# First attention: heads 8 to 15 of q turned in squares of 32 by VectorE and carried by transfers

## The chip, the core and the metric

The kernel runs on one core of a Trainium2 chip. The metric is the time of one execution on the device, in microseconds (us). A core has five engines that run side by side and wait for each other through semaphores: TensorE (PE; its loads of weights are PEld), VectorE (DVE), ScalarE (ACT), GpSimd (POOL) and SyncE (SP), which here only issues transfers (DMAs). TensorE runs at one of two clocks, 1.2 or 2.4 GHz; the profile gives the granted clock as a share of the higher.

## What is computed

Two transformer layers on 32 samples of 256 tokens by 128 features. The change is in the attention of the first layer, with 16 heads of q, 8 of k and v, 64 features a head:

```python
x = _rmsnorm(tokens, norm_w)
q = (x @ Wq).reshape(b, n, QH, DH).transpose(0, 2, 1, 3)
kv = x @ Wkv
...
q = _mh_rmsnorm(q, q_gamma)
k = _mh_rmsnorm(k, k_gamma)
g = QH // H
q = q.reshape(b, H, g, n, DH)
sim = jnp.einsum('bhgid,bhjd->bhgij', q, k)
sim = jnp.tanh(sim / SOFTCLAMP) * SOFTCLAMP
sim = sim * DH ** (-0.5)
...
attn = jax.nn.softmax(sim, axis=-1)
out = jnp.einsum('bhgij,bhjd->bhid', attn, v)
```

Before it stand a layer norm with a scale and a shift per sample, behind it a gated addition to x, then a mixture of experts, a second attention and a second feed-forward.

## The kernel before

Everything stays in the core's memory. `attention0` works sample by sample (n from 0 to 31); a sample is two tiles of 128 tokens (t = 0, 1). Each engine has its own order written out by hand in a loop over n, and a round of the loop mixes work of samples n - 1 to n + 3, so that the engines always have something of another sample.

For one sample: TensorE turns the normalised tokens (L314), projects q and k into three PSUM banks `pW` (L363, six blocks m = 0 to 5, f32), and v (L333). ScalarE squares each block (L761), VectorE multiplies it by a gain into `qg` (L582), sums the squares (L588), makes the factors (L603 to L622) and normalises (L629). Then q and k are split into two f16 halves, a high part by ScalarE (`act_hi`, L771) and the rest by `lower` (L643; k by VectorE, q by GpSimd), side by side in `kp` and `qp`, 64 + 64 columns a head. TensorE turns them, 128x128 at a time against the identity in `id16`: k in `pe_turn_k` (L375), q in `pe_turn_q` (L391), four groups i of eight heads (i = 2j + t, with j = 0 for heads 0 to 7 and j = 1 for heads 8 to 15). ScalarE copies k to `k1` (L777), VectorE q to `qs` (L651). SP copies `k1` with its halves exchanged to `k2` by two transfers (L306, L307).

The scores of a sample are four groups g of four heads (`pe_scores`, L407, eight matmuls each, called S0 to S3 in the text): q against `k1` and `k2`, summed in PSUM `pS`. S0 and S1 are heads 0 to 7, S2 and S3 heads 8 to 15. ScalarE takes tanh and exp of each group (L789, L795), GpSimd masks it (L864), TensorE multiplies by v for two heads at a time (`pe_weighted_values`, L422 and L423, p = 0 to 7), VectorE divides (L634, L638), GpSimd adds the two heads of a pair (L872). Pairs 6 and 7 of sample n - 1 are done after S0 of sample n. The turned heads go back through L444, L458 and L464 and are added to x.

Where q is turned in the order of the engines: i = 0 and 1 of sample n + 1 after S3 of sample n; i = 2 and 3 of sample n just after its S0, around pair 7 of sample n - 1. S0 waits for the copies of i = 0 and 1 and for `k2`, S2 for those of i = 2 and 3:

```python
if g == 0:
    pe.wait_ge(s_qs, 4 * n + 2)
    pe.wait_ge(s_k2, 32 * (n + 1))
elif g == 2:
    pe.wait_ge(s_qs, 4 * n + 4)
```

Of the kernel before, what the change touches and what calls it, by code (L numbers as in the profile page):

```python
# [241 lines left out]
def attention0(nc, c, weights):  # L242

    with ExitStack() as ctx:

# [3 lines left out]
        def sem(name):  # L251
# [8 lines left out]
        PAIRS = KH  # L260
        qp, kp = sb('qp', [P, TT, QH, 2 * DH], F16), sb('kp', [P, TT, KH, 2 * DH], F16)
        qs = [sb(f'qs{k}', [P, QH, N], F16) for k in range(2)]
        k1 = [sb(f'k1{k}', [P, KH, N], F16) for k in range(2)]
# [21 lines left out]
        BANK_OF = (0, 1, 2, 1, 0, 2)  # L285
        QT_BANK = (1, 0, 0, 2)
        SAMPLES_OF_LOAD = B // X_LOADS
# [3 lines left out]
            sem(x) for x in ('qk', 'sq', 'qg', 'ss', 'f', 'qn', 'hi', 'lo', 'ql'))  # L291
        s_qt, s_qs, s_kt, s_ks = (sem(x) for x in ('qt', 'qs', 'kt', 'ks'))
        s_k2, s_v, s_va = (sem(x) for x in ('k2', 'v', 'va'))
# [5 lines left out]
        @block.sync  # L299
        def _(sp):  # L300
            for n in range(B):
                k = n % 2
                if n >= 2:
                    sp.wait_ge(s_sc, 4 * (n - 1))
                sp.wait_ge(s_ks, 2 * n + 2)
                sp.dma_start(k2[k][0:DH, :, :], k1[k][DH:P, :, :]).then_inc(s_k2, 16)  # L306
                sp.dma_start(k2[k][DH:P, :, :], k1[k][0:DH, :, :]).then_inc(s_k2, 16)  # L307

        def pe_transpose_x(pe, n):
# [13 lines left out]
        def pe_values(pe, n, t):  # L323
            if t == 0:
                if n >= 1:
                    pe.wait_ge(s_qs, 4 * n)
                else:
                    pe.wait_ge(s_qg, 6)
            elif n + 1 < B:
                pe.wait_ge(s_qg, 6 * n + 7)  # L330
            else:
                pe.wait_ge(s_qs, 4 * n - 1)
            pe.matmul(pW[(2, 0)[t]][:, :], hT[n % 2][:, t * P:(t + 1) * P], wkv[:, KW:2 * KW], start=True, stop=True).then_inc(s_v, 1)  # L333

        def pe_project_qk(pe, n, m):
            if m == 0:
                pe.wait_ge(s_hT, n + 1)
                if n >= 2:
                    pe.wait_ge(s_qs, 4 * n - 5)
                elif n:  # L340
                    pe.wait_ge(s_qg, 5)
            elif m == 1:
                pe.wait_ge(s_msv, n + 1)
            elif m == 2:
                if n:
                    pe.wait_ge(s_va, 2 * n - 1)
            elif m == 3:
                if n:
                    pe.wait_ge(s_qs, 4 * n - 3)
                else:  # L350
                    pe.wait_ge(s_qg, 2)
            elif m == 4:
                if n:
                    pe.wait_ge(s_qs, 4 * n - 2)
# [22 lines left out]

        def pe_turn_q(pe, n, i):
            j, t = i // 2, i % 2
            if j == 0:  # L380
                pe.wait_ge(s_ql, 2 * n + t + 1)
                pe.wait_ge(s_ks, 2 * n + t + 1)
            elif n + 1 < B:
                pe.wait_ge(s_qg, 6 * n + 11 + t)
            elif t == 0:
                pe.wait_ge(s_qs, 4 * n + 2)
            else:
                pe.wait_ge(s_st, 4 * n - 7)
            out = pW[QT_BANK[i]][:, :].bitcast(F16)
            for h in range(KH):  # L390
                last = pe.transpose(out[:, h * P:(h + 1) * P], qp[:, t, j * KH + h, :], c.id16[:, :])  # L391
            last.then_inc(s_qt, 1)

        def pe_scores(pe, n, g):
            k = n % 2
            if g == 0:
                pe.wait_ge(s_qs, 4 * n + 2)
                pe.wait_ge(s_k2, 32 * (n + 1))
            elif g == 2:
                pe.wait_ge(s_qs, 4 * n + 4)  # L400
            if n or g:
                pe.wait_ge(s_th, 4 * n + g)
            for hh in range(0, HPG, G2):
                h = g * HPG + hh
                for out, keys in ((pS[:, hh * N:(hh + G2) * N], 0), (pS[:, HPG * N + hh * P:HPG * N + (hh + G2) * P], 1)):
                    for first, kk in ((True, k1[k]), (False, k2[k])):
                        last = pe.matmul(out, kk[:, h // G2, keys * P:(keys + 1) * P], qs[k][:, h:h + G2, keys * P:N], start=first, stop=not first)  # L407
            last.then_inc(s_sc, 1)
# [17 lines left out]
        def pe_heads_back(pe, n, t):  # L426
            if t == 0:
                pe.wait_ge(s_as, 8 * n + 8)
                if n + 3 < B:
                    pe.wait_ge(s_qg, 6 * n + 20)  # L430
                elif n + 3 == B:
                    pe.wait_ge(s_qg, 6 * B - 2)
                elif n + 2 == B:
                    pe.wait_ge(s_qs, 4 * B - 3)
                else:
                    pe.wait_ge(s_at, 2 * n - 1)
            elif n + 2 < B:
# [9 lines left out]
        def pe_out_project(pe, n):  # L447
            pe.wait_ge(s_at, 2 * n + 2)
            if n + 3 < B:
                pe.wait_ge(s_qg, 6 * n + 21)  # L450
            elif n + 3 == B:
                pe.wait_ge(s_va, 2 * B - 1)
            elif n + 2 == B:
                pe.wait_ge(s_qs, 4 * B)
            else:
                pe.wait_ge(s_st, 4 * n - 3)
# [116 lines left out]
        def dve_gain(dve, n, m):  # L573
# [66 lines left out]
        def lower(eng, n, u, t, done):  # L640
            eng.wait_ge(s_hi, 4 * n + 2 * u + t + 1)
            to, x = ((kp, qg[n % 2][:, t, QW:]), (qp, qg[n % 2][:, t, 0:QW]))[u]
            eng.tensor_tensor(to[:, t, :, DH:2 * DH], x.rearrange('p (h d) -> p h d', d=DH), to[:, t, :, 0:DH], ALU.subtract).then_inc(done, 1)  # L643

        def dve_take_q(dve, n, i):
            j, t = i // 2, i % 2
            dve.wait_ge(s_qt, 4 * n + i + 1)
            if i == 0 and n >= 2:
                dve.wait_ge(s_sc, 4 * n - 4)
            out = qs[n % 2][:, j * KH:(j + 1) * KH, t * P:(t + 1) * P]  # L650
            dve.tensor_copy(out, pW[QT_BANK[i]][:, :].bitcast(F16).rearrange('p (h i) -> p h i', i=P)).then_inc(s_qs, 1)  # L651

# [8 lines left out]
        def _(dve):  # L661
# [13 lines left out]
            for n in range(-3, B + 1):  # L675
# [7 lines left out]
                if 0 <= n < B:  # L683
                    dve_take_q(dve, n, 2)
                if 0 <= n + 1 < B:
# [3 lines left out]
                if 0 <= n < B:  # L689
                    dve_take_q(dve, n, 3)  # L690
                if 0 <= n + 1 < B:
# [71 lines left out]
        def act_hi(act, n, u, t):  # L763
            act.wait_ge(s_qn, 2 * n + t + 1)
            if n >= 1:
                if u:
                    act.wait_ge(s_qt, 4 * n - 1 + t)
                else:
                    act.wait_ge(s_kt, 2 * n - 1 + t)
            to, x = ((kp, qg[n % 2][:, t, QW:]), (qp, qg[n % 2][:, t, 0:QW]))[u]  # L770
            act.activation(to[:, t, :, 0:DH], x.rearrange('p (h d) -> p h d', d=DH), ACT.Copy).then_inc(s_hi, 1)  # L771

# [39 lines left out]
        def _(act):  # L812
# [3 lines left out]
            for n in range(-3, B + 1):  # L816
# [58 lines left out]
        def _(gp):  # L875
# [11 lines left out]
            for n in range(-1, B + 1):  # L887
# [1206 lines left out]
```

## Time and profile before

| | us |
|---|---|
| median of 3 runs | 2152.71 (2152.59 to 2153.12) |
| the profiled execution | 2151.95, its span 2150.1 |
| TensorE busy in the span | 2047.2 (95%) |
| VectorE, ScalarE, GpSimd busy | 1650.3 (77%), 1438.3 (67%), 618.3 (29%) |
| first attention, from the first scores to the last | 72.2 to 978.4 |

The profile is of one execution. Busy time is what an engine spent in instructions. A stretch is a piece of the span, given by its start and end. In the order of time a row is one group of like instructions of an engine, and square brackets behind it give the idle time before it and who ended it. Starts are in us from the start of the span.

### The profile page before, as it was taken

The numbers are of one execution on the slowest core, as the hardware profiler recorded it, in microseconds if no ns is written. First come the engines' busy times: TensorE is split into PE (matmuls) and PEld (weight loads), VectorE is DVE, ScalarE is ACT, GpSimd is POOL, SyncE is SP. The second block draws the span as 40 slices with busy tenths as digits, with TensorE's granted clock in tenths as the row PEclk, the third lists the DMA queues.
The fourth block names the chain that finished last, engine by engine and source line by source line (L and its number), as shares of the span: only waits on it lengthen the run. The fifth ranks groups of instructions, "written<-read, shape, count | busy, mean of one in ns | idle before, by whom it ended". The sixth has DMA issues, their size and how long they took to land. (4 is left out here: it accounts for less than half of the span.)

```text
span 2150.1 us, 40463 instructions
## 1 busy us (share of the span) xinstructions
PE 2047.2 (95%) x14885; PEld 1372.3 (64%) x14885; DVE 1650.3 (77%) x4015; ACT 1438.3 (67%) x1931; POOL 618.3 (29%) x862
## 2 busy tenths in 40 slices
PE   3899999999999999997999999799999996999998
PEld 1577777777777777775444444577777773444443
DVE  3888888888888888874566665577777776999997
ACT  1687877778887777873666666466666663555554
POOL 1345444544544454552000000133333331000000
PEclk9999999999999999997999999899999997999999
DMA  5000000000000000001000000000000000000000
GB/s 165 21 21 21 21 11 21 21 21 21 21 21 11 21 21 21 21 21 55 1 0 1 1 1 1 1 2 2 2 2 2 2 2 1 10 16 11 15 11 20
DMA packets 32834, 35.30 MB, mean 16 GB/s; under 512 B 6864, under 2 KB 26496, under 8 KB 32640
## 3 DMA queue, kind: packets, MB, share of 16 engines
q1 hardware_dynamic: 32640, 32.73, 5.8%
q8 instruction: 120, 1.97, 0.4%
q14 instruction: 74, 0.61, 0.1%
HBM read 11.75 MB, written 4.19 MB: 7 GB/s over the span
## 5 line engine op out<-in xcount | busy, mean ns | idle before, releaser
L864 POOL TENSOR_SCALAR_AFFINE_SELECT pr<-pr 128x512 f32<-128x512 f32 x256 | 202.2, 813 | 370.7 <-ACT pr L795 370.7
L422 PE MATMUL a_pO<-va,pr 128*128 128x66 f32 x2048 | 304.6, 272 | 1.9 <-POOL pr L864 1.5
L422 PEld LDWEIGHTS a_pO<-va,pr 128*128 128x128 f32 x2048 | 273.7, 193 | 18.9 <-issue 15.4
L1628 ACT ACTIVATE c_pr<-c_pS 128x1536 f32<-128x1536 f32 x128 | 186.0, 1453 | 119.3 <-PE c_pS L1440 119.3
L1683 POOL TENSOR_SCALAR_AFFINE_SELECT c_pr<-c_pr 128x512 f32<-128x512 f32 x256 | 158.0, 641 | 265.4 <-DVE c_pr L1548 265.4
L761 ACT ACTIVATE sq<-a_pW 128x512 f32<-128x512 f32 x192 | 114.4, 597 | 145.4 <-PE a_pW L363 142.7
L789 ACT ACTIVATE th<-a_pS 128x1536 f32<-128x1536 f32 x128 | 185.9, 1453 | 30.1 <-PE a_pS L407 29.6
L423 PE MATMUL a_pO<-va,pr 128*128 128x66 f32 x1024 | 199.0, 276 | 0.0
L795 ACT ACTIVATE pr<-th 128x1536 f32<-128x1536 f32 x128 | 190.5, 1488 | 3.1
L407 PE MATMUL a_pS<-qs,k 128*128 128x512 f16 (+1 forms) x1024 | 187.3, 326 | 0.9 <-issue 0.9
L1548 DVE TENSOR_SCALAR c_pr<-c_pr 128x1536 f32<-128x1536 f32 x128 | 122.6, 958 | 78.4 <-ACT c_pr L1628 78.4
L1021 PE MATMUL b_pU<-b_hT,b_uT 128*128 128x512 f32 x320 | 168.8, 610 | 0.0
L1039 PE MATMUL b_pD<-b_a,b_dT 128*128 128x512 f32 x320 | 163.1, 593 | 0.0
L407 PEld LDWEIGHTS a_pS<-qs,k 128*128 128x128 f16 x1024 | 98.7, 98 | 99.7 <-issue 35.9
L1187 DVE TENSOR_TENSOR b_a<-b_q,b_pC 128x512 f32<-128x512 f32 x128 | 87.8, 686 | 96.1 <-ACT b_q L1271 96.0
L1258 ACT ACTIVATE b_r<-b_pU 128x512 f32<-128x512 f32 x160 | 95.4, 596 | 95.6 <-PE b_pU L1021 95.6
L423 PEld LDWEIGHTS a_pO<-va,pr 128*128 128x128 f32 x1024 | 156.6, 193 | 0.0
L872 POOL TENSOR_TENSOR as<-on 128x128 f32<-128x128 f32 x256 | 116.6, 466 | 109.7 <-PE a_pW L444 95.0
L643 POOL TENSOR_TENSOR qp<-qg,qp 128x1024 f16<-128x1024 f32 x64 | 136.7, 2137 | 25.2 <-ACT qp L771 25.2
L582 DVE TENSOR_TENSOR qg<-a_pW,a_gam 128x512 f32<-128x512 f32 x192 | 131.4, 685 | 10.5 <-ACT sq L761 7.9
L634 DVE RECIPROCAL rl<-a_pO 128x4 f32<-128x4 f32 x256 | 45.0, 176 | 120.5 <-PE a_pO L423 120.5
L363 PE MATMUL a_pW<-a_wq,hT 128*128 128x512 f32 x256 | 125.7, 615 | 1.3 <-DVE qs L651 0.7
(259 smaller groups left out, 4509.1 us busy)
## 6 DMA issues: line engine op xcount, KB each, us to landing
k<-k SPq DMA_DIRECT2D x64, 256.0 KB, 3.6
x<-in_L_attn_tokens_dram SPq DMA_DIRECT2D x8, 512.0 KB, 6.8
out_dram<-x SPq DMA_DIRECT2D x16, 256.0 KB, 2.3
d_h<-in_L_ffn_h_w_dram SPq DMA_DIRECT2D x2, 1024.0 KB, 7.4
wmod<-in_L_wmod_dram SPq DMA_DIRECT2D x2, 384.0 KB, 4.0
d_w<-in_L_ffn_w_w_dram SPq DMA_DIRECT2D x3, 256.0 KB, 3.2
a_wq<-in_L_attn_Wq_dram SPq DMA_DIRECT2D x1, 512.0 KB, 7.1
a_wkv<-in_L_attn_Wkv_dram SPq DMA_DIRECT2D x1, 512.0 KB, 6.9
```

What stands on the lines that cost most here:

```text
L407: last = pe.matmul(out, kk[:, h // G2, keys * P:(keys + 1) * P], qs[k][:, h:h + G2, keys * P:N], start=first, stop=not first)
L422: pe.matmul(out, w[:, hh * N + t * P:hh * N + (t + 1) * P], v[:, 0, p, :], start=True, stop=t == 0)
L423: last = pe.matmul(out, w[:, HPG * N + hh * P:HPG * N + (hh + 1) * P], v[:, 1, p, :], start=False, stop=True)
L582: dve.tensor_tensor(qg[n % 2][:, t, cols], pW[BANK_OF[m]][:, :], gam[:, cols], ALU.mult).then_inc(s_qg, 1)
L643: eng.tensor_tensor(to[:, t, :, DH:2 * DH], x.rearrange('p (h d) -> p h d', d=DH), to[:, t, :, 0:DH], ALU.subtract).then_inc(done, 1)
L789: act.activation(th[:, :], pS[:, :], ACT.Tanh, scale=1.0 / SOFTCLAMP).then_inc(s_th, 1)
L795: act.activation(pr[g % 2][:, :], th[:, :], ACT.Exp, scale=SOFTCLAMP * DH ** (-0.5)).then_inc(s_pr, 1)
L864: last = gp.affine_select(out=part, in_=part, compare_op=ALU.is_ge, fill=0.0, base=0, pattern=[[0, HPG], [1, P]], channel_multiplier=-1)
L1021: pe.matmul(pU[u % 2][:, :], uT[:, t * P:(t + 1) * P], hT[n % 2][:, :], start=True, stop=True).then_inc(s_up, 1)
L1039: pe.matmul(pD[:, :], dT[:, t * D:(t + 1) * D], a[(IT * n + u) % 4][:, :], start=u == 0, stop=u == IT - 1).then_inc(s_dn, 1)
L1628: act.activation(pr[g][:, :, :], pS[:, :, 0:N + P], ACT.Exp, scale=float(1.0 / np.sqrt(np.float32(DQ)))).then_inc(s_ex, 1)
L1683: last = gp.affine_select(out=part, in_=part, compare_op=ALU.is_ge, fill=0.0, base=0, pattern=[[0, HPG], [1, P]], channel_multiplier=-1)
```

## The change

TensorE no longer turns heads 8 to 15 of q. Their high and low halves go to a new tile `qr`, laid out in four pieces of 32 columns (g = 0, 1 the high part, g = 2, 3 the low one) with the eight heads side by side, 8 x 32 columns each. VectorE turns each 32 x 32 square of a tile of tokens in place (`dve_turn_q`, one instruction for 128x1024), into `qt`. What stands then in the 32 partitions j are the 32 columns of each piece; SP carries piece g of partitions j to partitions 32g of a new tile `qd` with 16 transfers of 32 partitions x 2 x 256 f16, 32 KB each. The scores of heads 8 to 15 read `qd`, in pieces of 32 queries. Each step of high and low parts is now three instructions a tile of tokens (k, q 0 to 7, q 8 to 15) instead of two. S2 waits for the 16 transfers. Several waits for PSUM banks become shorter, because `pW` is used for two turns of q less.

```diff
+                sp.wait_ge(s_rt, 2 * n + 2)
+                for j in range(S4):
+                    for g in range(S4):
+                        sp.dma_start(qd[k][32 * g:32 * (g + 1), j::S4, :], qt[32 * j:32 * (j + 1), :, g, :]).then_inc(s_qd, 16)
...
         def pe_scores(pe, n, g):
             k = n % 2
             if g == 0:
-                pe.wait_ge(s_qs, 4 * n + 2)
+                pe.wait_ge(s_qs, 2 * n + 2)
                 pe.wait_ge(s_k2, 32 * (n + 1))
             elif g == 2:
-                pe.wait_ge(s_qs, 4 * n + 4)
+                pe.wait_ge(s_qd, 256 * (n + 1))
...
+                    if h < KH:
+                        queries = qs[k][:, h:h + G2, keys * P:N]
+                    else:
+                        queries = qd[k][:, keys * S4:, (h - KH) * 32:(h - KH + G2) * 32].rearrange('p j (h i) -> p h j i', h=G2)
...
+        def dve_turn_q(dve, n, t):
+            dve.wait_ge(s_ql, 4 * n + 2 + t + 1)
+            if n >= 1 and t == 0:
+                dve.wait_ge(s_qd, 256 * n)
+            dve.transpose(qt[:, t, :, :].rearrange('p g r -> p (g r)'), qr[:, t, :, :].rearrange('p g r -> p (g r)')).then_inc(s_rt, 1)
...
                 if 0 <= n < B:
-                    dve_take_q(dve, n, 2)
+                    dve_turn_q(dve, n, 0)
...
                     act_hi(act, n + 1, 1, 1)
+                    act_hi(act, n + 1, 2, 0)
                     act_take_k(act, n + 1, 0)
+                    act_hi(act, n + 1, 2, 1)
                     act_take_k(act, n + 1, 1)
```

In TensorE's order, after S0 (L407 before, L414 now), this stood between the first scores of a sample and the projections of sample n + 2:

```order
L320 MATMUL a_pW<-ones,hsq 128x1 x2
L391 MATMUL a_pW<-id,qp 128x128 x8
L422 MATMUL a_pO<-va,pr 128x66 x2
L423 MATMUL a_pO<-va,pr 128x66
...
L391 MATMUL a_pW<-id,qp 128x128 x8
L363 MATMUL a_pW<-a_wq,hT 128x512 x2
```

and now stands:

```order
L336 MATMUL a_pW<-ones,hsq 128x1 x2
L429 MATMUL a_pO<-va,pr 128x66 x2
L430 MATMUL a_pO<-va,pr 128x66
...
L374 MATMUL a_pW<-a_wq,hT 128x512 x2
L414 MATMUL a_pS<-qs,k 128x512 x2
```

The sixteen turns are gone; pairs 6 and 7 and the projections follow each other directly.

VectorE's order at the same place of the round, before:

```order
L571 TENSOR_SCALAR ss<-a_pW 128x2
L651 COPY qs<-a_pW 128x8x128
L603 TENSOR_SCALAR rr<-ss 128x52
...
L634 RECIPROCAL rl<-a_pO 128x4
L638 TENSOR_TENSOR on<-a_pO,rl 128x256
L651 COPY qs<-a_pW 128x8x128
L612 SCALAR_TENSOR_TENSOR rr<-rt,rr 128x52
```

and now:

```order
L572 TENSOR_SCALAR ss<-a_pW 128x2
L658 STREAM_TRANSPOSE qt<-qr 128x1024
L604 TENSOR_SCALAR rr<-ss 128x52
...
L635 RECIPROCAL rl<-a_pO 128x4
L639 TENSOR_TENSOR on<-a_pO,rl 128x256
L658 STREAM_TRANSPOSE qt<-qr 128x1024
L613 SCALAR_TENSOR_TENSOR rr<-rt,rr 128x52
```

The turns stand in the places of the two copies, the second behind the outputs of pair 7.

SP's queue of one sample, which was L306 and L307 alone:

```order
L309 DMA k<-k 64x2048
L310 DMA k<-k 64x2048
L314 DMA qd<-qt 32x2x256 x16
L309 DMA k<-k 64x2048
L310 DMA k<-k 64x2048
```

The sixteen transfers of sample n stand between the exchange of k of sample n and that of sample n + 1.

## Rows read from the trace of the kernel before

**Rows 1.** Busy time by stretch: stretch, its length, engines with instruction counts, clock, DMA.

```profile
400.00:700.00 300.00, 300.00 (x2244) 231.74 (x2243) 258.70 (x577) 242.76 (x284) 147.99 (x189) 1.00 0.08 19
```

**Rows 2.** TensorE in order of time, one sample: start, length, engine, line, tiles.

```profile
503.40 1.46 PE L407 MATMUL a_pS<-qs,k 128*128 128x512 f16 x8
...
506.40 0.61 PE L391 MATMUL a_pW<-id,qp 128*128 128x128 f16 x8
506.85 0.61 PE L422 MATMUL a_pO<-va,pr 128*128 128x66 f32 x4
...
508.19 0.61 PE L391 MATMUL a_pW<-id,qp 128*128 128x128 f16 x8
508.63 1.94 PE L363 MATMUL a_pW<-a_wq,hT 128*128 128x512 f32 x4
...
517.40 1.46 PE L407 MATMUL a_pS<-qs,k 128*128 128x512 f16 x8
...
532.31 1.46 PE L407 MATMUL a_pS<-qs,k 128*128 128x512 f16 x8
```

**Rows 3.** VectorE in order of time, after the first scores of that sample.

```profile
504.80 1.74 DVE L588 TENSOR_REDUCE ss<-sq 128x24 f32<-128x1536 f32 x1
...
507.07 0.68 DVE L651 COPY qs<-a_pW 128x1024 f16<-128x1024 f16 x1
...
509.37 0.42 DVE L638 TENSOR_TENSOR on<-a_pO,rl 128x256 f32<-128x256 f32 x1
509.71 0.68 DVE L651 COPY qs<-a_pW 128x1024 f16<-128x1024 f16 x1
```

**Rows 4.** ScalarE's copies of k, SP's two transfers behind them, L307's landing.

```profile
523.45 2.17 ACT L777 ACTIVATE k<-a_pW 128x1024 f16<-128x1024 f16 x2
...
525.69 0.46 SPq L306 DMA_DIRECT2D k<-k  x1
526.20 0.60 SPq L307 DMA_DIRECT2D k<-k  x1
...
DMA to landing us min/median/max: 3.5/3.7/4.7
```

**Rows 5.** Other issues of SP: order of time, L1773's durations, table with landing times.

```profile
21.03 0.43 SPq L1360 DMA_DIRECT2D c_up<-in_L_attn_W_UQ_dram  x1
21.50 0.42 SPq L1361 DMA_DIRECT2D c_up<-in_L_attn_W_UK_dram  x1
...
L1773 SPq DMA_DIRECT2D out_dram<-x x16: 372/373/399, 1849.9 to 2147.4; - x16
...
out_dram<-x SPq DMA_DIRECT2D x16, 256.0 KB, 2.3
...
c_kr<-in_L_attn_W_KR_dram SPq DMA_DIRECT2D x1, 2.0 KB, 2.1
```

**Rows 6.** Stretches of 2 us at the stage's entry, and TensorE in order of time.

```profile
58.00:60.00 2.00, 0.00 (x0) 0.00 (x0) 2.00 (x3) 0.94 (x3) 0.00 (x0) 1.00 0.00 0
60.00:62.00 2.00, 0.62 (x8) 0.45 (x8) 1.82 (x7) 2.00 (x4) 0.07 (x1) 0.81 0.00 0
...
70.00:72.00 2.00, 2.00 (x4) 0.80 (x3) 0.98 (x2) 0.60 (x1) 0.00 (x0) 0.63 0.00 0
...
67.32 3.73 PE L363 MATMUL a_pW<-a_wq,hT 128*128 128x512 f32 x4
```

**Rows 7.** One stretch near the end of the stage.

```profile
960.00:962.00 2.00, 1.05 (x9) 0.72 (x9) 1.53 (x6) 0.59 (x1) 1.34 (x3) 1.00 0.29 102
```

**Rows 8.** ScalarE and GpSimd in order of time: high parts, a low part, a mask.

```profile
517.37 0.63 ACT L771 ACTIVATE kp<-qg 128x512 f16<-128x512 f32 x1
...
522.50 1.07 ACT L771 ACTIVATE qp<-qg 128x1024 f16<-128x1024 f32 x1
...
521.57 2.14 POOL L643 TENSOR_TENSOR qp<-qg,qp 128x1024 f16<-128x1024 f32 x1
...
528.93 1.22 POOL L864 TENSOR_SCALAR_AFFINE_SELECT pr<-pr 128x512 f32<-128x512 f32 x2 [1.12 <-ACT pr L795]
```

More of the change, by code:

```diff
@@ L260, in attention0 @@
         PAIRS = KH
-        qp, kp = sb('qp', [P, TT, QH, 2 * DH], F16), sb('kp', [P, TT, KH, 2 * DH], F16)
-        qs = [sb(f'qs{k}', [P, QH, N], F16) for k in range(2)]
+        S4, SQ = P // 32, KH * 32
+        qp, kp = (sb(x, [P, TT, KH, 2 * DH], F16) for x in ('qp', 'kp'))
+        qr, qt = (sb(x, [P, TT, S4, SQ], F16) for x in ('qr', 'qt'))
+        qs = [sb(f'qs{k}', [P, KH, N], F16) for k in range(2)]
+        qd = [sb(f'qd{k}', [P, TT * S4, SQ], F16) for k in range(2)]
         k1 = [sb(f'k1{k}', [P, KH, N], F16) for k in range(2)]
@@ L291, in attention0 @@
             sem(x) for x in ('qk', 'sq', 'qg', 'ss', 'f', 'qn', 'hi', 'lo', 'ql'))
-        s_qt, s_qs, s_kt, s_ks = (sem(x) for x in ('qt', 'qs', 'kt', 'ks'))
+        s_qt, s_qs, s_kt, s_ks, s_rt, s_qd = (sem(x) for x in ('qt', 'qs', 'kt', 'ks', 'rt', 'qd'))
         s_k2, s_v, s_va = (sem(x) for x in ('k2', 'v', 'va'))
@@ L307, in _, with halves @@
                 sp.dma_start(k2[k][DH:P, :, :], k1[k][0:DH, :, :]).then_inc(s_k2, 16)
+                sp.wait_ge(s_rt, 2 * n + 2)
+                for j in range(S4):
+                    for g in range(S4):
+                        sp.dma_start(qd[k][32 * g:32 * (g + 1), j::S4, :], qt[32 * j:32 * (j + 1), :, g, :]).then_inc(s_qd, 16)
+        def halves(n, u, t):
+            if u == 2:
+                return tuple(qr[:, t, g:g + S4 // 2, :].rearrange('p g (h i) -> p h g i', i=32) for g in (0, S4 // 2)) + (
+                    qg[n % 2][:, t, KW:QW].rearrange('p (h g i) -> p h g i', g=S4 // 2, i=32),)
+            to = (kp, qp)[u]
+            x = (qg[n % 2][:, t, QW:], qg[n % 2][:, t, 0:KW])[u]
+            return to[:, t, :, 0:DH], to[:, t, :, DH:], x.rearrange('p (h d) -> p h d', d=DH)
         def pe_transpose_x(pe, n):
@@ L324, in pe_values @@
             if t == 0:
[L325 to L328, printed above, removed]
+                pe.wait_ge(s_qg, 6 * n + 6)
             elif n + 1 < B:
@@ L337, in pe_project_qk @@
                 pe.wait_ge(s_hT, n + 1)
[L338 to L341, printed above, removed]
+                if n:
+                    pe.wait_ge(s_qg, 6 * n - 1)
             elif m == 1:
@@ L348, in pe_project_qk @@
                 if n:
-                    pe.wait_ge(s_qs, 4 * n - 3)
+                    pe.wait_ge(s_qs, 2 * n - 1)
                 else:
@@ L353, in pe_project_qk @@
                 if n:
-                    pe.wait_ge(s_qs, 4 * n - 2)
+                    pe.wait_ge(s_qs, 2 * n)
                 else:
@@ L376, in pe_turn_k, with pe_turn_q @@
             last.then_inc(s_kt, 1)
[L378 to L385, printed above, removed]
-                pe.wait_ge(s_qs, 4 * n + 2)
-            else:
-                pe.wait_ge(s_st, 4 * n - 7)
-            out = pW[QT_BANK[i]][:, :].bitcast(F16)
+        def pe_turn_q(pe, n, t):
+            pe.wait_ge(s_ql, 4 * n + t + 1)
+            pe.wait_ge(s_ks, 2 * n + t + 1)
+            out = pW[1 - t][:, :].bitcast(F16)
             for h in range(KH):
-                last = pe.transpose(out[:, h * P:(h + 1) * P], qp[:, t, j * KH + h, :], c.id16[:, :])
+                last = pe.transpose(out[:, h * P:(h + 1) * P], qp[:, t, h, :], c.id16[:, :])
             last.then_inc(s_qt, 1)
@@ L405, in pe_scores @@
                 for out, keys in ((pS[:, hh * N:(hh + G2) * N], 0), (pS[:, HPG * N + hh * P:HPG * N + (hh + G2) * P], 1)):
+                    if h < KH:
+                        queries = qs[k][:, h:h + G2, keys * P:N]
+                    else:
+                        queries = qd[k][:, keys * S4:, (h - KH) * 32:(h - KH + G2) * 32].rearrange('p j (h i) -> p h j i', h=G2)
                     for first, kk in ((True, k1[k]), (False, k2[k])):
-                        last = pe.matmul(out, kk[:, h // G2, keys * P:(keys + 1) * P], qs[k][:, h:h + G2, keys * P:N], start=first, stop=not first)
+                        last = pe.matmul(out, kk[:, h // G2, keys * P:(keys + 1) * P], queries, start=first, stop=not first)
             last.then_inc(s_sc, 1)
@@ L433, in pe_heads_back @@
                 elif n + 2 == B:
-                    pe.wait_ge(s_qs, 4 * B - 3)
+                    pe.wait_ge(s_qs, 2 * B - 1)
                 else:
@@ L439, in pe_heads_back @@
             elif n + 2 == B:
-                pe.wait_ge(s_qs, 4 * B - 1)
+                pe.wait_ge(s_qs, 2 * B)
             else:
@@ L640, in lower, with dve_take_q @@
         def lower(eng, n, u, t, done):
[L641 to L648, printed above, removed]
-                dve.wait_ge(s_sc, 4 * n - 4)
-            out = qs[n % 2][:, j * KH:(j + 1) * KH, t * P:(t + 1) * P]
-            dve.tensor_copy(out, pW[QT_BANK[i]][:, :].bitcast(F16).rearrange('p (h i) -> p h i', i=P)).then_inc(s_qs, 1)
+            eng.wait_ge(s_hi, 6 * n + 2 * u + t + 1)
+            hi, lo, x = halves(n, u, t)
+            eng.tensor_tensor(lo, x, hi, ALU.subtract).then_inc(done, 1)
+        def dve_take_q(dve, n, t):
+            dve.wait_ge(s_qt, 2 * n + t + 1)
+            if t == 0 and n >= 2:
+                dve.wait_ge(s_sc, 4 * n - 4)
+            out = qs[n % 2][:, :, t * P:(t + 1) * P]
+            dve.tensor_copy(out, pW[1 - t][:, :].bitcast(F16).rearrange('p (h i) -> p h i', i=P)).then_inc(s_qs, 1)
+        def dve_turn_q(dve, n, t):
[3 more added lines that the diff above has]
+            dve.transpose(qt[:, t, :, :].rearrange('p g r -> p (g r)'), qr[:, t, :, :].rearrange('p g r -> p (g r)')).then_inc(s_rt, 1)
         def dve_add(dve, n):
@@ L689, in _ @@
                 if 0 <= n < B:
-                    dve_take_q(dve, n, 3)
+                    dve_turn_q(dve, n, 1)
                 if 0 <= n + 1 < B:
@@ L765, in act_hi @@
             if n >= 1:
[L766 to L771, printed above, removed]
+                act.wait_ge((s_kt, s_qt, s_rt)[u], 2 * n - 1 + t)
+            hi, _, x = halves(n, u, t)
+            act.activation(hi, x, ACT.Copy).then_inc(s_hi, 1)
         def act_take_k(act, n, t):
@@ L906, in _ @@
                     gp_sum(gp, n, 3)
+                if 0 <= n + 1 < B:
+                    lower(gp, n + 1, 2, 0, s_ql)
+                    lower(gp, n + 1, 2, 1, s_ql)
                 if 0 <= n < B:
```

13 lines of the change are left out of this document (2 added, 11 removed).

## The prediction

> **What bounds the kernel now.** The changed stage is the first attention: 32 samples from about 72 to 982 us of a span of 2150.1 us. I first read the table of stretches: between 400 and 700 us TensorE is busy 300.00 of 300 us at a granted clock of 1.00, VectorE 258.70, ScalarE 242.76, GpSimd 148 [rows 1]. TensorE is the bound, and its order of time shows it with no gap. There I take the first score group of two samples in a row, the eight L407 matmuls that start at 503.40 and at 532.31: one sample costs 28.91 us, and 32 of them 925 us [rows 2]. All times below are counted from 503.40, called S0. The third score group, S2, starts at 517.40, so at 14.00; from there to the next S0 lie 14.91 us of unbroken TensorE work. S2 is the group to watch, because in the new kernel it is the first that reads heads 8 to 15.
>
> **What leaves TensorE.** Eight turns of q start at 506.40 and what follows starts at 506.85: 0.45 us. Eight more start at 508.19, and all sixteen belong to heads 8 to 15 [rows 2]. So 0.89 us leave each sample, both pieces between S0 and S2, and S2 could start at 13.11. If nothing else waited, the period would be 28.02 and the gain 32 x 0.89 = 28.5 us.
>
> **What VectorE does instead.** Its two copies of L651 at 507.07 and 509.71 (0.68 us each, from PSUM) become two 32 x 32 turns of 128x1024 f16 in the same two places [rows 3]. The trace before has no such turn. Between the copy, 0.68 us, and the reduction of 128x1536, 1.74 us [rows 3], I take the reduction's rate per element, 1024/1536 x 1.74 = 1.16 us, since a turn has to stream every element through; the ends are 0.68 and 1.74. The second one started at 509.71, so at 6.31; the first one before it is now 0.48 longer, so 6.79, and it ends at 7.95. It can't come earlier, because VectorE runs without a gap there, and what stands before it (the outputs of head pair 7) needs TensorE's work after S0. The Trainium skill ("VectorE: DVE Perf Modes", The three transpose paths) gives 311 ns for one 128x128 in bf16; an estimate by that page would be 8 x 311 = 2.49 us for ours, two of them 2.66 us more than my sum has and 85 us over 32 samples; no run here shows it yet.
>
> **What SP's queue does now, the term that decides.** After the second turn SP issues 16 transfers of 32 KB, one after another, and S2 waits for all 256 counts. From the end of ScalarE's copies (525.62) to SP's issue at 525.69 is 0.07 us; the next issue starts at 526.20, so 0.51 us from one issue to the next [rows 4]. That pair is the nearest row, both are SBUF to SBUF. The ends: stores to out_dram take 0.373 us, with the 0.05 between issues 0.42; small loads stand 0.47 apart (21.03 and 21.50) [rows 5]; the second transfer of k takes 0.60, with the 0.05 it would be 0.65 [rows 4]. Fifteen steps of 0.51 are 7.65. From issue to landing the same table has 2.1 us for 2 KB, 2.3 for 256 KB in runs of 512 B; the second transfer of k, 256 KB in runs of 4 KB, has 3.7 [rows 4, 5]; ours are 32 KB in runs of 512 B, so 2.3. Sum: 7.95 + 0.07 + 7.65 + 2.3 = 17.97 us. TensorE is ready for S2 at 13.11, so it stands idle 4.86 us in each sample. The period becomes 17.97 + 14.91 = 32.88 us, 3.97 over 28.91: 32 x 3.97 = 127 us lost. The 28.5 us gained are inside this sum and vanish in the wait. The Trainium skill ("DMA: Bandwidth & Descriptors", Rules for kernel authors) speaks against such a change: under 64 KB a transfer is mostly overhead, one should merge them. The row on c_kr, 2 KB in 2.1 us beside 256 KB in 2.3, agrees.
>
> **What the idle does to TensorE's clock.** This kernel has one such place to look at, the entry to the stage. TensorE did nothing from 58 to 60 us and little from 60 to 62, and the granted clock went from 1.00 (2.4 GHz) to 0.50 (1.2 GHz); it stayed there, and came back only near 71.5 (0.63 over the stretch 70 to 72), after TensorE had worked from 67.32 on without a gap [rows 6]. The four L363 of that stretch took 3.73 us; the same four at full clock take 1.94 (508.63) [rows 2, 6]. About 4 us at half speed cost 1.9 us of work. A shorter pause, 960 to 962 with 1.05 of 2 us busy, left the clock at 1.00 [rows 7]. A pause of 4.9 us of nothing is longer than the first of these, so I expect the fall in nearly every sample: 1.9 us each, 61 us in all, with ends at 0 and at twice that. The Trainium skill ("TensorE: Matmul & The Clock Gate", HAM oscillation) describes this pattern, a wait for a transfer in each round of a loop that brings the clock down each time.
>
> **What else moves, at nothing.** ScalarE's high parts go from 2 x 1.07 us to four of about 0.63 [rows 8], 0.4 us more a sample; half of them now stand before the copies of k, so the transfers of k and the following turns of q go out up to 0.8 us later after S2. The transfer of k lands at 526.20 + 3.7 = 529.9 and is needed at 532.31 [rows 2, 4], 2.4 us of cover. GpSimd's low parts (2.14 us for 1024) become four of half the size [rows 8]; two stand ahead of the mask of group 3, which ended at 530.15 and is needed after the next S0, over 3 us later [rows 8, 2]. The earlier part of the round, where VectorE is 1 us longer, is covered by the idle time before S2; were that gone, this 1 us would stand against 0.89 us of saving and about eat it. SP's 16 issues end near 16 and k's next issue is due at 22.3 (525.69 - 503.40), so they don't meet. The score matmuls of groups 2 and 3 read q in pieces of 32 elements instead of 128 and more; I take no cost, the other end is twice their time, 2 x 1.3 us a sample (83 us).
>
> **The sum.** 2151.95 (the profiled execution) + 127 + 61 = 2340; the median of the runs is 0.8 us above that execution, so **2341 us**.
>
> **Rivals.** (a) The wait for transfers without the fall of the clock: 2152.7 + 127 = **2280**. For it: the stage has no pause between busy stretches that shows a fall from full load, and the fall at 61 us came after a thin ten microseconds. (b) All transfers hidden, the side of faster: the 16 land before 13.11, so within 5.09 us of the end of the second turn. With 2.3 us to land that wants (5.09 - 2.3)/15 = 0.19 us an issue; no issue in the trace is below 0.37. It gives 2152.7 - 28.5 = **2124**. The break-even, S2 at 14.00, wants 0.25 us an issue. (c) The chain is longer than I have it: issues 0.65 apart add 15 x 0.14 = 2.1 us a sample, 67 us, **2408**; the pieces of 32 in the score matmuls, 2341 + 83 = **2424**. Beside it stands the page on VectorE's turns: by its figure, an estimate, 2341 + 85 = 2426. As a mechanism of this kernel it is the same as the others of (c), since all that comes before the sixteenth landing adds to the period one for one.
>
> **How the numbers follow.** Forecast 0.56, (a) 0.21, (b) 0.07, (c) 0.16. The low end goes below (a) with issues 0.47 apart and 2.1 to land (0.6 + 0.2 = 0.8 us less a sample, 26 us): 2254, and a little more for a shorter turn, 2245. The high end takes in one of the terms of (c): 2420. About 0.2%, 4 us, is what a measurement of this kernel can tell from no change. Faster 0.06, the same 0.02 (a break-even is a narrow hit between 2124 and 2280), slower 0.92.
>
> **What would show it.** In the new profile S2 (first score group on qd) starts some 18 us after S0, with 4.9 us of idle before it that ends with a transfer; SP's issues of qd stand 0.5 us apart, 2.3 us to landing; VectorE's turns take 1.2 us; the period is 34 to 35 us, with half of some 4 us after S2 at clock 0.50; TensorE's busy share in 400:700 falls to near 85%. I am wrong if the issues take less than 0.25 us each, or if S2 starts within 14 us of S0.

## The result and the profile after

The changed kernel takes 2501.3 us (median of 4 runs, 2494.7 to 2508.0) where the kernel before takes 2152.7: a ratio of 1.162 (95% interval 1.159 to 1.165), 349 us slower. The sign and the place of the loss were forecast; the size, 2341 us and at most 2420, was not.

The same table of stretches as [rows 1], of the changed kernel (stretch, length, busy time of PE, PEld, DVE, ACT and POOL, granted clock, share of the DMA engines, GB/s). The second row is one sample, from S0 to S0, then its pieces: the wait before S2, the stretch after it, and the rest.

```profile
400.00:700.00 300.00, 248.95 (x1483) 186.11 (x1482) 193.64 (x423) 179.29 (x218) 100.13 (x150) 0.85 0.11 27
509.12:549.33 40.21, 33.87 (x202) 25.67 (x200) 25.43 (x57) 23.99 (x30) 13.49 (x20) 0.83 0.11 27
522.90:528.95 6.05, 0.00 (x0) 0.00 (x1) 5.07 (x11) 1.63 (x3) 0.00 (x0) 0.81 0.20 49
528.95:541.00 12.05, 12.05 (x52) 10.16 (x53) 2.43 (x6) 6.00 (x7) 5.84 (x9) 0.53 0.00 0
541.00:549.33 8.33, 8.33 (x67) 6.19 (x66) 4.53 (x13) 5.45 (x7) 3.60 (x6) 1.00 0.26 65
```

TensorE had 300.00 of 300 us before, now 248.95, and the clock is 0.85 on average. One sample takes 40.21 us instead of 28.91. Two pieces are new: 6.05 us in which TensorE does nothing, and 12.05 us behind them at nearly half clock (0.53), although TensorE is busy in all of them. The same sample in TensorE's order of time (start, length, line, tiles, in brackets the idle time before and who ended it), beside [rows 2]:

```profile
509.12 1.46 PE L414 MATMUL a_pS<-qs,k 128*128 128x512 f16 x8
...
521.41 0.63 PE L451 MATMUL a_pW<-id,as 128*128 128x128 f32 x4 [0.28 <-DVE qg L583]
521.87 1.02 PE L374 MATMUL a_pW<-a_wkv,hT 128*128 128x512 f32 x2
528.95 2.74 PE L414 MATMUL a_pS<-qd,k 128*128 128x512 f16 x8 [6.05 <-DMA qd<-qt]
...
541.45 1.46 PE L414 MATMUL a_pS<-qd,k 128*128 128x512 f16 x8
...
549.33 1.46 PE L414 MATMUL a_pS<-qs,k 128*128 128x512 f16 x8
```

S2 starts 19.83 us after S0 (14.00 before) and is ended by the transfers of qd. From S2 to the next S0 it takes 20.38 us (14.91 before). S2 itself takes 2.74 us at half clock, S3, the same work at full clock, 1.46 as before. VectorE and SP in the same sample, beside [rows 3] and [rows 4], and the page's table of issues (KB each, median us to landing), beside [rows 5]:

```profile
512.61 1.23 DVE L658 STREAM_TRANSPOSE qt<-qr 128x1024 f16<-128x1024 f16 x1
...
516.09 1.23 DVE L658 STREAM_TRANSPOSE qt<-qr 128x1024 f16<-128x1024 f16 x1
...
517.35 10.28 SPq L314 DMA_DIRECT2D qd<-qt  x16
...
qd<-qt SPq DMA_DIRECT2D x512, 32.0 KB, 1.9
```

The second turn ends at 517.32, 8.20 after S0. Sixteen issues take 10.28 us, 0.643 each. The last lands 1.9 us after its issue.

Over the stage: S0 of sample 1 starts at 109.53 and S0 of sample 31 at 1307.08, so the mean period is (1307.08 - 109.53)/30 = 39.92 us, 11.0 more than 28.91, times 32 = 352 us. (The span of this execution is 356 us longer, 2506.3 against 2150.1.) Of the 11.0 us the later start of S2 has 5.9 (19.89 on average, 14.00 before) and the time from S2 to the next S0 has 5.1 (20.02 on average, 14.91 before): 188 and 164 us. The stages behind are unchanged: from the last score group to the end of the span it is 1173 us in both kernels.

### The profile page after: what moved, and what is told of

It is laid out like the page before. It is cut to its first block and busy times, and to the rows that moved or that the text cites. A ratio compares the mean times of both kernels' runs of the same rounds, so it can differ in the third digit from the quotient of the medians.

```text
span 2506.3 us, 40172 instructions
## 1 busy us (share of the span) xinstructions
PE 2195.8 (88%) x14373; PEld 1463.4 (58%) x14373; DVE 1664.8 (66%) x4015; ACT 1460.7 (58%) x1995; POOL 604.3 (24%) x926
## 5 line engine op out<-in xcount | busy, mean ns | idle before, releaser
L429 PE MATMUL a_pO<-va,pr 128*128 128x66 f32 x2048 | 350.5, 301 | 2.9 <-POOL pr L870 2.0
L429 PEld LDWEIGHTS a_pO<-va,pr 128*128 128x128 f32 x2048 | 321.7, 223 | 21.8 <-issue 17.0
L414 PE MATMUL a_pS<-qd,k 128*128 128x512 f16 (+1 forms) x512 | 135.9, 428 | 201.5 <-DMA qd<-qt 201.5
L870 POOL TENSOR_SCALAR_AFFINE_SELECT pr<-pr 128x512 f32<-128x512 f32 x256 | 178.8, 722 | 402.5 <-ACT pr L799 402.5
L430 PE MATMUL a_pO<-va,pr 128*128 128x66 f32 x1024 | 224.6, 306 | 0.0
L414 PEld LDWEIGHTS a_pS<-qd,k 128*128 128x128 f16 x512 | 57.4, 120 | 282.7 <-DMA qd<-qt 226.8
L430 PEld LDWEIGHTS a_pO<-va,pr 128*128 128x128 f32 x1024 | 181.7, 222 | 0.0
L639 DVE TENSOR_TENSOR on<-a_pO,rl 128x256 f32<-128x256 f32 x256 | 108.7, 425 | 47.1 <-POOL as L878 39.1
```

The costliest lines, as they stand in the source:

```text
L429: pe.matmul(out, w[:, hh * N + t * P:hh * N + (t + 1) * P], v[:, 0, p, :], start=True, stop=t == 0)
L430: last = pe.matmul(out, w[:, HPG * N + hh * P:HPG * N + (hh + 1) * P], v[:, 1, p, :], start=False, stop=True)
L870: last = gp.affine_select(out=part, in_=part, compare_op=ALU.is_ge, fill=0.0, base=0, pattern=[[0, HPG], [1, P]], channel_multiplier=-1)
```

## Experiments

Twelve kernels were run. Where an edit says "changed kernel", it starts from the kernel after. Runs with fewer transfers leave out a part of q of heads 8 to 15, as their expectations say.

### The clock: needless work in the wait

```diff
             elif g == 2:
+                pe.wait_ge(s_th, 4 * n + g)
+                for _ in range(4):
+                    # eight score matmuls of heads 0 to 3 into pS, which S2 overwrites
                 pe.wait_ge(s_qd, 256 * (n + 1))
```

> The changed kernel plus 32 needless score matmuls a sample on TensorE (heads 0 to 3 four times over, into the bank that S2 overwrites), placed where TensorE waits for the transfers; some 5.2 us of the 6.05 us of idle are filled. Nothing else is changed. Theory 1, the idle time brings the clock down: S2 stays at 19.8 us after S0, from S2 to the next S0 it is 14.9 us again instead of about 21, the period is 34.8 and the kernel takes about 2340 us, faster than the changed kernel by 160 us although TensorE does more. Rival, the stretch after S2 is slow for another reason (q read in pieces of 32, copies and turns colliding): the period stays at 40 and the time at 2500 us, or longer if the filler delays S2.

Measured: 2376.8 us (ratio to before 1.104, 1.096 to 1.111). That is 125 us faster than the changed kernel, with 32 matmuls a sample more. The row of its middle stretch:

```profile
400.00:700.00 300.00, 286.66 (x1988) 207.95 (x1987) 213.46 (x468) 200.67 (x246) 115.09 (x170) 1.00 0.13 31
```

The clock is 1.00 from sample 0 to sample 28 (it fell in the last three), most periods are 35.0 to 36.3 us, and 0.8 to 2.1 us of idle are left. The total is 37 us above the 2340 of the theory, since these waits vary and S2 to S0 takes 15.18 us, not 14.9. The rival is gone: nothing in the reading of `qd` and nothing in the work behind S2 is slow by more than this 0.27 us, and the idle time brings the clock down. The transfers, the issues and the 19.8 us are still there, and they alone cost some 6 us a sample.

### How many transfers: 8, 12, 14 and none

```diff
-                        sp.dma_start(qd[k][32 * g:32 * (g + 1), j::S4, :], ...)
+                        if n < 2 or S4 * j + g < CARRIED:
+                            sp.dma_start(qd[k][32 * g:32 * (g + 1), j::S4, :], ...)
```

> The changed kernel with only 8 of the 16 transfers from the third sample on; the other half of qd keeps the first samples' data, so the scores of heads 8 to 15 are left incomplete. Theory, the chain of issues sets S2: turn ends at 8.2 after S0, 7 x 0.643 to the last issue, 1.9 to land: S2 at 14.7, idle about 1 us, clock stays at 1.00, period 29.6, total about 2195 us (the first two samples keep 16 transfers). Rival, any wait brings the clock down: period 31.5 to 35, 2250 to 2360 us.

> The changed kernel with 12 of the 16 transfers from the third sample on (a part of qd keeps the first samples' data). Chain: 8.23 + 11 x 0.643 + 1.95 = 17.25 us, idle before S2 3.4 us. If the clock stayed up: period 32.2, total about 2275 us. Theory, the clock falls at this length of idle too, as before the stage: the stretch from S2 to the next S0 is 17 to 21 us in most samples, period 34 to 38, total 2340 to 2450 us. Rival, it falls only with the 6 us of idle: 2275 us.

> The changed kernel with 14 of the 16 transfers from the third sample on (a part of qd keeps the first samples' data). S2 comes at 8.23 + 13 x 0.643 + 1.95 = 18.5 us, idle 4.8 us. It asks what makes the stretch at half clock long (some 6 us lost a sample with 6 us of idle) or short (1.9 us lost with 3.5 us of idle). Theory, the longer the idle the longer TensorE stays at half clock: between, 3 to 4.5 us lost, period 36.5 to 38, total 2420 to 2465 us. Rival, two kinds of outage only, and their mix shifts: periods of 35.3 and of 39.5 side by side in the trace, total in the same range or above.

> The changed kernel without any of the 16 transfers from the third sample on (heads 8 to 15 are scored from the first samples' q). It shows what the turns taken from TensorE are worth alone. Theory, TensorE is the bound: the period is 28.91 - 0.89 = 28.0 to 28.3 us, total about 2150 to 2158 us with the first two samples as slow as before. Rival, VectorE with its longer turns becomes the bound in the middle of the round: the period stays at 28.9, about 2177 us.

| transfers | idle before S2, us | typical period, us | total, us | ratio to before (95%) |
|---|---|---|---|---|
| 16 (changed kernel) | 6.05 | 40.9, some 36.3 to 37.1 | 2501.3 | 1.162 (1.159 to 1.165) |
| 14 | 4.8 | 35.4 and 39.5 in turn | 2430.5 | 1.129 (1.127 to 1.131) |
| 12 | 3.5 | 34.1 | 2332.3 | 1.083 (1.081 to 1.085) |
| 8 | 0.9 | 29.9 | 2218.7 | 1.030 (1.027 to 1.033) |
| 0 | none | 28.78 | 2172.2 | 1.009 (1.006 to 1.012) |

The idle times follow the sum to 0.1 us: each transfer left out takes 0.64 us. With 8 the clock stays up in samples 2 to 29. (The total is 24 us above the 2195 expected; the clock fell in the first two samples, which keep 16 transfers, and in the last two.) With 12 it falls in every sample, but for 3.4 us only in nearly all, and S2 to S0 comes to 34.1 - 17.25 = 16.85 us, 1.9 more than before. With 8 transfers, at clock 1.00, this stretch is 15.17 us, so 0.26 of the 1.9 is not the clock. The total lies just under the range I gave, which took in longer falls. With 14 there are two kinds of sample side by side, as the rival of that run had it. TensorE at 12 transfers, then at 14 (a sample with a long fall, and one with a short):

```profile
464.00:467.40 3.40, 0.00 (x0) 0.00 (x0) 3.37 (x11) 1.63 (x3) 0.00 (x0) 0.97 0.20 48
467.43:470.50 3.07, 3.07 (x12) 1.78 (x12) 1.61 (x1) 0.30 (x1) 0.00 (x0) 0.50 0.00 0
470.50:475.50 5.00, 5.00 (x42) 4.72 (x43) 2.22 (x6) 4.45 (x6) 3.18 (x6) 0.99 0.00 0
```

```profile
310.51:323.00 12.49, 12.49 (x52) 10.49 (x53) 2.78 (x7) 6.00 (x7) 6.28 (x10) 0.50 0.00 0
...
385.50:388.50 3.00, 2.97 (x12) 1.69 (x13) 0.36 (x1) 0.20 (x1) 0.00 (x0) 0.55 0.00 0
388.50:393.00 4.50, 4.50 (x41) 4.34 (x41) 2.22 (x6) 4.20 (x6) 2.83 (x5) 1.00 0.02 4
```

The run without transfers was the surprise. With nothing to wait for, the period is 28.78 us, 0.13 below before and not the 0.89 that left TensorE. (The total is above before because the first two samples keep 16 transfers and cost 14 us more, and the last two cost some 8 us more, the last one largely at clock 0.50.) Its TensorE and VectorE in order of time show one of the places:

```profile
325.71 1.07 PE L352 MATMUL a_pW<-a_wkv,hT 128*128 128x512 f32 x2
...
327.08 0.63 PE L457 MATMUL a_pW<-id,as 128*128 128x128 f32 x4 [0.29 <-DVE qg L589]
```

```profile
321.75 1.24 DVE L664 STREAM_TRANSPOSE qt<-qr 128x1024 f16<-128x1024 f16 x1
...
324.58 1.75 DVE L636 TENSOR_TENSOR qg<-qg,rr 128x1536 f32<-128x1536 f32 x1
326.25 0.68 DVE L589 TENSOR_TENSOR qg<-a_pW,a_gam 128x512 f32<-128x512 f32 x1
```

From v's second projection to the turn of the heads back it was 0.92 us before (515.19 to 516.11), it is 1.37 now: VectorE's gain of block 1, which frees the bank, ends at 326.93. That it is late because the two turns take 1.23 us each for copies of 0.68 is argued from the order, not tested alone. A second piece, 0.21 us, stands ahead of the k projection of block 5, where the profile names VectorE's addition to x. It lies behind S2, and the samples of the changed kernel with a long fall of the clock don't have it.

### VectorE's gain of block 1 earlier

```diff
+                if 0 <= n + 2 < B:
+                    dve_gain(dve, n + 2, 1)
                 if 0 <= n + 1 < B:
                     dve_norm(dve, n + 1, 0)
-                if 0 <= n + 2 < B:
-                    dve_gain(dve, n + 2, 1)
```

> The run without the transfers (28.78 us a sample, 2172 us) with one more edit: VectorE's gain of block 1 of sample n + 2 stands ahead of its normalisation of sample n + 1, so the bank that the turns of the heads back wait for is free 1.7 us earlier. Theory, 0.3 to 0.45 us of the 0.89 us taken from TensorE are lost in that wait on VectorE: the wait goes, the period is 28.35, about 2159 us. Rival, VectorE's total work is the bound: period 28.8, 2172 us.

Measured: 28.71 us a sample, only 0.07 less; the total is unclear (4 runs from 2159.4 to 2171.0). The wait named in the theory did go (S2 starts 13.14 us after S0 instead of 13.62), and another took its place behind S2 (S2 to S0 15.57 instead of 15.16):

```profile
PE a_pW L469 <- ACT at L811: 3.1, 10, 0.3
```

(the waits of 400 to 700 us: who waited for whom, us in total, times, longest). ScalarE copies the turned heads 0.3 us too late for TensorE, and before that copy it waits for VectorE's normalisation. So it is not one wait but, it seems, VectorE's whole order after S0 that takes back the saving. Both my theory and the rival were half right.

### Half as many rows in each transfer

```diff
+                        if n < 2: (as before)
+                        else:
+                            sp.dma_start(qd[k][32 * g:32 * (g + 1), j, :], qt[32 * j:32 * (j + 1), 0, g, :]).then_inc(s_qd, 16)
```

> The changed kernel with 16 transfers a sample that carry only the first tile of tokens from the third sample on: 32 rows of 512 B each instead of 64; the second tile's part of qd keeps the first samples' data. It measures what sets the 0.643 us from issue to issue. Theory, a fixed cost per transfer: it stays at 0.64, S2 at 19.8, total about 2490 to 2500 us. Rival, the cost goes with the rows of a transfer: about 0.5 us or less, S2 at 17.7 or earlier, period shorter by 2 us, about 2430 us or less.

Measured: 2461.6 us (1.143, 1.141 to 1.145), idle 5.75 us. From the trace, SP in order of time and the durations of the line (ns, least, median, most):

```profile
384.86 10.04 SPq L317 DMA_DIRECT2D qd<-qt  x16
...
L317 SPq DMA_DIRECT2D qd<-qt x480: 507/591/1365, 150.6 to 1277.0; - x160
DMA to landing us min/median/max: 1.7/1.8/2.7
```

Sixteen issues take 10.04 us instead of 10.28, with half the rows and half the bytes. The cost is one per transfer, 0.63 to 0.64 us; of the ways to lower it, fewer transfers (above) and a second queue (below) were tried, larger merged ones were not. The total lies below my 2490 because more samples have a short outage of the clock (periods of 36 to 37 us: 12 of samples 2 to 29, against 5 in the changed kernel); that the 0.3 us less of idle is the reason wasn't shown.

### What makes a fall long: half the filler

The filler of the first experiment, with 2 rounds instead of 4.

> The changed kernel with half the filler of the earlier run: 16 needless score matmuls a sample, 2.6 us, all 16 transfers kept. S2 stays at 19.8 us, the idle time is 3.5 us as in the run with 12 transfers. Theory, the loss at half clock hangs on the idle time alone: 1.9 us a sample as there, period 36.7, total about 2400 us. Rival, it hangs on the transfers in flight or on what follows: period near 40 as with 16 transfers and no filler, 2480 us or more.

Measured: 2530.2 us (1.175, 1.173 to 1.177), slower than with no filler at all. My theory of the idle time alone falls: this run has the same 3.4 to 3.5 us of idle in most samples as the one with 12 transfers, but nearly each fall is long. One sample of it:

```profile
533.00:536.43 3.43, 0.00 (x0) 0.00 (x1) 2.50 (x5) 0.00 (x0) 0.00 (x0) 0.84 0.20 48
536.43:548.50 12.07, 12.07 (x51) 10.24 (x52) 2.42 (x6) 6.00 (x7) 5.86 (x9) 0.50 0.01 1
548.50:556.00 7.50, 7.50 (x64) 5.81 (x63) 3.26 (x9) 4.64 (x5) 3.44 (x6) 0.97 0.28 70
```

The clock was down already 1.1 us before S2 (0.84 over 3.43 us of idle; with 12 transfers 0.97 over 3.40, so down only 0.2 us before). The length goes with the moment of the fall. Of samples 0 to 29 of five runs (16, 14 and 12 transfers, half the rows, half the filler), 50 had a fall between 0.76 us before the start of S2 and 0.5 us after it, and the clock was back after 3.41 us; 82 had it 0.78 to 2.27 us before, and it stayed low for 13.65 us; 15 had it 2.4 to 3.2 us before, with 6.83 us; the last 3, all with half the filler, had it 0.6 to 0.8 us after the start of S2, with 10.24 us. What sets the moment of the fall within the wait wasn't settled.

### What makes a fall long: what follows it

```diff
-            for hh in range(0, HPG, G2):
+            for hh in (hh for _ in range(3 if g == 2 else 1) for hh in range(0, HPG, G2)):
```

> The changed kernel with the third score group computed three times in a row with the same result: 16 needless matmuls a sample directly behind the wait for the transfers, 2.6 us at full clock. All 16 transfers and the 6 us of idle stay. With 6 us of idle the clock stayed low for some 13.6 us in most samples, 6.1 us lost, though TensorE had no gap after S2. Theory, what TensorE does right after the wait sets how long the clock stays low: with large matmuls there it comes back within 3 to 7 us, and although 2.6 us are added the stretch from S2 to the next S0 is about 20 to 21 us as before, total 2480 to 2510 us. Rival, the outage has its length whatever follows: S2 to S0 is 23.7 us, total near 2585 us.

Measured: 2511.0 us (1.167, 1.163 to 1.170), 10 us above the changed kernel with 83 us (32 x 2.6) of needless work in it. One sample:

```profile
528.78:533.50 4.72, 4.72 (x15) 2.14 (x16) 0.00 (x0) 0.00 (x0) 0.00 (x0) 0.50 0.01 3
533.50:535.50 2.00, 2.00 (x11) 1.05 (x10) 0.00 (x0) 0.00 (x0) 0.00 (x0) 0.69 0.00 0
535.50:541.30 5.80, 5.80 (x55) 5.50 (x53) 2.21 (x6) 5.21 (x6) 3.65 (x7) 1.00 0.00 0
```

With 6.05 us of idle as before, the clock is back 6.0 us after S2 began, not 12. In none of the 32 samples did it stay low for longer than that after S2. In 18 of them the clock fell 0.78 to 2.27 us before S2, where all 82 samples of the runs above had an outage of 13.65 us; here it is 6.83 us in all 18. So, at the same moment of the fall, the length hangs on what TensorE does right behind the wait: with 24 score matmuls there the clock came back, with 8 of them and then the many small ones of the weighted values and of the turns (128x66 and 128x128) TensorE was busy and stayed at half clock. It is not the only thing: the short outages above ended behind the same 8 score matmuls.

### The turns earlier

```diff
+                if 0 <= n < B:
+                    dve_turn_q(dve, n, 0)
+                    dve_turn_q(dve, n, 1)
                 if 0 <= n + 1 < B:
                     dve_gain(dve, n + 1, 5)
-                    dve_sums(dve, n + 1, 1)
                 (outputs of pair 6, mean square)
+                if 0 <= n + 1 < B:
+                    dve_sums(dve, n + 1, 1)
```

> The changed kernel with both of VectorE's turns moved ahead of its gain of block 5, where their inputs lie ready, and the sums moved behind the mean square; all 16 transfers stay. Theory, each us that the second turn comes earlier moves S2 by one us: the turn ends 2.7 us after S0 instead of 8.2, S2 starts at 14.3, the idle time is 1.2 us, the clock stays at 1.00, the period is 29.2 and the total about 2162 us. Rivals: the clock falls at this wait too, period 31 to 35, 2220 to 2350 us; or the 2.5 us ahead of gain 5 stall TensorE at another place (projection 1, pair 0), period about 30, 2190 us.

Measured: 2220.3 us (1.031, 1.028 to 1.035), 58 us above the theory and at the low edge of its first rival. The turns end 3.0 us after S0 instead of 8.2 and S2 starts at 14.6 instead of 19.8: 5.2 us earlier gave 5.2 us. The idle time is some 1.25 us in 12 of samples 1 to 29, with a period of 29.8, and up to 2.4 us in others. In 5 of samples 1 to 29 the clock fell, after waits of 2.0 to 2.4 us, with periods of 32.2 to 35.6. The mechanism holds; the size was off, since the waits vary and some still bring the clock down.

### A second queue, and a kernel that beats both

The early turns, the early gain, and 3 of the 16 transfers issued by ScalarE behind its first exp (13 by SP; S2 waits for both queues):

```diff
                     act_exp(act, n, 0)
+                    if n >= 2:
+                        act.wait_ge(s_sc, 4 * (n - 1))
+                    act.wait_ge(s_rt, 2 * n + 2)
+                    for i in range(13, 16):
+                        j, g = i // S4, i % S4
+                        act.dma_start(qd[n % 2][32 * g:32 * (g + 1), j::S4, :], qt[32 * j:32 * (j + 1), :, g, :]).then_inc(s_qe, 16)
```

> A kernel that computes everything: VectorE's turns early (ahead of its gain of block 5), gain of block 1 ahead of the normalisation, and 3 of the 16 transfers issued by ScalarE behind its first exp, 13 by SP. Theory: SP's chain ends at 2.7 + 12 x 0.643 + 1.95 = 12.4 us after S0, before TensorE wants S2 at 13.2; no idle, no fall of the clock, period 28.3 to 28.5, total 2130 to 2140 us, faster than both kernels. Rival, ScalarE's 1.9 us of issuing or the moved turns stall TensorE at another place: period 28.9 to 29.5, 2150 to 2175 us.

Measured: 2146.7 us, ratio 0.9973 (0.9961 to 0.9985): faster than the kernel before by 0.3%, and not the 2130 to 2140 us of the theory. The period is 28.3 us in most samples and S2 waits less than 0.5 us from sample 1 to 29, but the last two samples, whose rounds are shorter, wait 2.2 and 3.4 us and lose their clock. So the next has 4 transfers on ScalarE, and 8 in these two samples.

> The kernel with early turns and the earlier gain again, with 4 of the 16 transfers issued by ScalarE and 8 in the last two samples, where the round is shorter and the first version waited 2.2 and 3.4 us and lost its clock. Theory: these two waits shrink below 1 us and the clock stays up, 5 to 8 us less than the first version: 2139 to 2142 us, 0.5 to 0.6% faster than the kernel before. Rival: ScalarE's eight issues (5 us) delay its squares and its tanh in the last rounds by as much as they save: 2144 to 2150 us.

Measured: 2141.1 us (5 runs, 2139.5 to 2145.6), ratio 0.9946 (0.9932 to 0.9960), 12 us or 0.5% below the kernel before. The two waits shrank to nothing and 1.0 us, but in the profiled execution the clock didn't stay up: behind S2 of sample 30 TensorE waited 2.0 us for GpSimd's mask and then ran 10.2 us at half clock. In order of time and by stretch:

```profile
327.86 7.72 SPq L323 DMA_DIRECT2D qd<-qt  x12
...
327.92 2.84 ACTq L842 DMA_DIRECT2D qd<-qt  x4
...
324.80 1.46 PE L424 MATMUL a_pS<-qs,k 128*128 128x512 f16 x8
...
337.94 1.46 PE L424 MATMUL a_pS<-qd,k 128*128 128x512 f16 x8
...
400.00:700.00 300.00, 300.00 (x2121) 227.43 (x2120) 262.96 (x596) 246.37 (x308) 151.19 (x215) 1.00 0.16 39
```

S2 follows 13.14 us after S0, where I had put its earliest start (13.11), without a wait. The period is 28.29: 0.62 of the 0.89 us are kept. What each of the three edits gives of this was not separated, beyond the run with the early turns alone.

## Why the prediction was wrong

**The bound and the place: right.** The chain turn, issues, landing, S2 sets the period, as the forecast said; no other wait of note appeared. That the second turn can't come earlier held only for VectorE's order as written: another order brought it 5.2 us forward. Of this chain the turn (1.16 forecast, 1.23 measured) and the landing (2.3 against 1.9) were near. The Trainium skill ("VectorE: DVE Perf Modes", The three transpose paths) would have put a turn at 2.49 us, an estimate by its figure of 311 ns for one 128x128 in bf16; the trace differs, 1.23 us, and the measurement decides. S2 in pieces of 32 costs nothing (1.46 us as before). The rival of hidden transfers did not come, and would have given 4 us, not 28.5.

**The step that failed first: 0.51 us from issue to issue.** It is 0.643. I took the step from the first to the second transfer of k, which holds the 0.46 us of L306; L307, of the same size, has 0.60, and with the 0.05 between issues 0.65, in the same group [rows 4]. I had this row as the upper end. It was the right one, and not because an issue behind another costs more: the first of the sixteen goes into an idle queue and takes 0.64 us.

```profile
517.35 0.64 SPq L314 DMA_DIRECT2D qd<-qt  x1
```

Why L306 is cheaper, no run here shows. The step makes 15 x 0.13 = 2.0 us a sample; the turn ended 0.25 later and the landing took 0.4 less than forecast, so S2 is at 19.83 instead of 17.97: 60 us of the 160 missed. The rows of the transfers had next to no part in it, as the run with half of them shows.

**The step that failed most: 1.9 us for the clock.** From S2 to the next S0 it came to 5.1 us a sample more than before (20.4 to 21.1 us in most samples, 16.5 to 17.3 in some), 3.2 us or 103 us in all above the forecast. A small part of it, 0.27 us in the samples with a short outage, is the wait on VectorE behind S2 and not the clock. The fall itself and its cause were right, which the filler shows. The size came from one place, the entry to the stage, and from a part of it. The clock was at 0.50 there from 61.2 to 71.5 us, 10.2 us; I costed only the last 4, the four L363 [rows 6], since TensorE had done turns with pauses before them. In the loop TensorE has no pause behind S2, so all of the outage costs, and in most samples it lasts until 11.4 to 12.9 us after S2 began. Even twice my term, the upper end, would have been too low. The trace before had a nearer row, just behind the stage, though the forecast says that there is one such place only:

```profile
982.83:996.48 13.65, 11.14 (x40) 9.28 (x40) 1.77 (x8) 1.49 (x3) 1.91 (x5) 0.50 0.00 0
```

Here, too, small matmuls follow a pause (1.50 us, then weighted values of 128x66), the clock is at 0.50 for 13.65 us, and TensorE is busy in 11.14 of them. Half of that, 5.6 us a sample, would have given, as an estimate, 2152.7 + 127 + 179 = 2459 us. The Trainium skill ("TensorE: Matmul & The Clock Gate", HAM oscillation) has the pattern, a wait in each round that brings the clock down; the trace agrees, with a fall to 0.50 at the wait of all 32 samples.

**The gain in hand: 28.5 us was too much.** It was lost in the wait and so did not matter for the result, but as a number it was wrong: without any transfer the period falls by 0.13 us, 4 us in all. I had written that VectorE's extra 1 us stood against the 0.89, and would "about eat it"; that was right, and should have gone into the rival's time, 2149 instead of 2124. With VectorE's turns and its gain of block 1 at other places and a part of the issues on ScalarE, 0.62 us a sample can be had.

## What to carry to other kernels

Cost a row of small transfers by issue time, times their number, on one queue. Of two issues of the same kind take the dearer: here it was the right one. Half the bytes and rows changed the time by 2%. The chain starts at the last thing that its first issue waits for. Before TensorE is left idle in a loop, count the clock as well: in these runs it fell at every wait before S2 of 3.4 us or more, at some of 2.0 to 2.4 us, and at none that was shorter, though behind the stage it fell after shorter pauses too (1.5 us, above). Cost all the time at half clock in which TensorE has work, and look for every place in the trace where the clock fell. What runs right after the wait changes how long it stays low, and needless matmuls in the wait can pay (32 a sample did, 16 made it worse). Moving the start of such a chain to where its inputs are ready, and a part of the issues to a second queue, turned a loss of 16% into a gain of 0.5%.

## What the runs showed of the hardware

TensorE can be busy in 12.07 of 12.07 us and stay at clock 0.50 (the run with half the filler), and come back 3.4 us after the fall elsewhere (12 transfers) with the same idle time of 3.5 us ahead of it. An issue of a transfer costs SP 0.63 to 0.64 us in a row of sixteen, whether it carries 32 or 64 rows, and ScalarE's queue 0.71 (2.84 us for 4). The first of the sixteen costs as much as the others (0.64); the first of the two transfers of k costs less, 0.46 before and 0.51 after. A 128x1024 f16 turn in squares of 32 takes VectorE 1.23 us.
